# Window attention on one core: softmax over half sequences, keys without padding, rstd per sequence

## What is computed

```python
def _L1_attn_ref(x, wq, wk, wv, wo, q_norm_w, k_norm_w):
    DIM, H, KV, HD, WIN = (128, 16, 4, 64, 64)
    def rmsnorm(x, w, eps=1e-06):
        return x * jax.lax.rsqrt(jnp.mean(x * x, axis=-1, keepdims=True) + eps) * w
    q = rmsnorm((x @ wq.T).reshape(B, T, H, HD), q_norm_w)
    k = rmsnorm((x @ wk.T).reshape(B, T, KV, HD), k_norm_w)
    v = (x @ wv.T).reshape(B, T, KV, HD)
    k = jnp.repeat(k, rep, axis=2); v = jnp.repeat(v, rep, axis=2)
    scores = jnp.einsum('bqhd,bkhd->bhqk', q, k) / jnp.sqrt(jnp.float32(HD))
    mask = (i >= j) & (i - j < WIN)
    attn = jax.nn.softmax(jnp.where(mask, scores, -jnp.inf), axis=-1)
    y = jnp.einsum('bhqk,bkhd->bqhd', attn, v).reshape(B, T, H * HD)
    return y @ wo.T
```

## Time and profile before

| | |
|---|---|
| median of 3 runs | 2810.6 us (2810.01 to 2815.29) |
| the profiled execution | 2811.5 us, its span 2809.7 us |
| mean granted TensorE clock | 0.949 |
| busy over the span: PE, PEld | 2401.2 us (85%), 1568.5 us (56%) |
| busy over the span: DVE, ACT, POOL | 2138.4 (76%), 1455.2 (52%), 1191.9 us (42%) |
| the window attention layer | about 1754 to 2272 us of the span |

### The profile page before, as it was taken

One profiled execution on the slowest core, in us unless ns is written; L12 is line 12 of the kernel. 1 busy time (PEld: TensorE's weight loads), 2 busy tenths in 40 slices (PEclk: granted clock), 3 DMA queues, 4 the chain that ended last, 5 costly groups with the idle time before them and its releaser, 6 DMA issues. The chain is left out here.

```text
span 2809.7 us, 46598 instructions
## 1 busy us (share of the span) xinstructions
PE 2401.2 (85%) x14880; PEld 1568.5 (56%) x14880; DVE 2138.4 (76%) x3085; ACT 1455.2 (52%) x2617; POOL 1191.9 (42%) x864
## 2 busy tenths in 40 slices
PE   2778878778887877799779999699999989978997
PEld 0233333333333332577578888466666767767776
DVE  3899999999999999577555555588888867764555
ACT  2666666666666774466332222466666646642010
POOL 4566667666666667333300000455555533231000
PEclk9899999999999999899789999899999999988999
DMA  2000000000000000200000000000000010000000
GB/s 84 1 0 0 1 0 1 1 1 0 0 0 0 0 1 0 63 12 12 22 1 1 1 0 0 6 0 0 0 0 0 1 48 11 11 4 1 11 7 12
DMA packets 35414, 22.17 MB, mean 8 GB/s; under 512 B 22710, under 2 KB 34017, under 8 KB 34801
## 3 DMA queue, kind: packets, MB, share of 16 engines
q1 hardware_dynamic: 35312, 20.98, 2.9%
HBM read 18.87 MB, written 2.10 MB: 7 GB/s over the span
## 5 line engine op out<-in xcount | busy, mean ns | idle before, releaser
L784 POOL TENSOR_TENSOR m_hc<-m_h,m_cs 128x1024 f32<-128x1024 f32 x256 | 603.2, 2359 | 351.9 <-DVE m_h L706 344.6
L706 DVE TENSOR_TENSOR_SCAN m_h<-m_da,m_pdb 128x1024 f32<-128x1024 f32 x256 | 585.1, 2286 | 23.5 <-DVE m_pdb L661 5.0
L456 PE MATMUL m_py<-m_hc,ident 128*128 128x512 f32 x1024 | 514.6, 627 | 4.2 <-DVE m_y L670 2.1
L579 ACT ACTIVATE m_da<-m_dt,m_aneg 128x508 f32<-128x508 f32 x512 | 337.8, 709 | 47.8 <-POOL m_dt L753 46.1
L661 DVE TENSOR_TENSOR m_pdb<-m_du,m_pdb 128x1024 f32<-128x1024 f32 x256 | 314.8, 1230 | 42.7 <-POOL m_du L760 11.4
L456 PEld LDWEIGHTS m_py<-m_hc,ident 128*128 128x128 f32 x1024 | 202.2, 200 | 213.6 <-issue 174.6
L594 ACT ACTIVATE m_cs<-m_pc 128x512 f32<-128x512 f32 x256 | 150.5, 588 | 219.7 <-PE m_pc L446 219.6
L442 PE MATMUL m_pdb<-m_bcrow,m_sel 96*128 96x512 bf16 x256 | 101.8, 397 | 171.8 <-DVE m_h L706 170.8
L1391 ACT ACTIVATE c_act_of<-c_pg 128x512 f32<-128x512 f32 x144 | 86.2, 598 | 237.3 <-PE c_pg L212 237.3
L1759 POOL TENSOR_TENSOR d_pr<-d_pr,d_rden 128x512 f32<-128x512 f32 x128 | 133.3, 1041 | 177.2 <-DVE d_rden L1690 177.2
L1037 ACT ACTIVATE x_prT<-x_pt 77x512 f32<-77x512 f32 x256 | 137.8, 587 | 130.6 <-PE x_pt L939 129.5
(11 more groups left out here) (257 smaller groups left out, 5373.7 us busy)
## 6 DMA issues: line engine op xcount, KB each, us to landing
cw_gu<-in_C_gu SPq DMA_DIRECT2D x1, 2304.0 KB
x<-in_x SPq DMA_DIRECT2D x8, 256.0 KB, 4.9
fw_w<-in_F_w SPq DMA_DIRECT2D x1, 2048.0 KB
out_x<-x SPq DMA_DIRECT2D x8, 256.0 KB, 2.3
bm_mrow<-in_B_mrow SPq DMA_DIRECT2D x1, 1232.0 KB, 6.5
x_ctxT<-in_B_ctxT SPq DMA_DIRECT2D x32, 38.5 KB, 1.8
x_mask<-in_B_mrow SPq DMA_DIRECT2D x32, 38.5 KB, 2.8
x_ctxT<-in_E_ctxT SPq DMA_DIRECT2D x32, 38.5 KB, 1.8
```

Source lines behind the costliest of these rows:

```text
L456: ins = mm(py[:, c, :], S.ident[:, :], hc[n % BUF][:, place(n, c), :], start=n == 0, stop=n == NS - 1)
L579: A_(dst, src, ACT.Exp, scale=aneg[:, d, c, n:n + 1]).then_inc(s["da_ready"], 1)
L706: V.tensor_tensor_scan(h[n % BUF][:, way], da[n % BUF][:, d:d + CH * GT][:, way], pdb[:, b:b + 2, :].rearrange("p c t -> p (c t)")[:, way] ...
L784: P.tensor_tensor(hc[n % BUF][:, :, :], h[n % BUF][:, :].rearrange("p (c t) -> p c t", c=CH), bc(cs[n % BUF][:, :], 1, CH), ALU.mult).then ...
```

## The change

The layer is rewritten with halves (8 heads) in place of quads.

- **Softmax by half sequences.** Maximum, subtraction, exp, sum, reciprocal and normalization work on 128 x 1024 elements, twice per sequence. pr becomes four buffers of 1024, top, den and rden two of 8 columns.
- **Scores in row tiles.** kT is copied in one instruction without padding. ps is one tensor of two banks, both used by each half: heads in rows 0 to 63 go to bank 0, heads in rows 64 to 127 to bank 1, eight products of 64 rows and 128 columns per half, the two row halves in turn. Scores of a half wait for the subtraction of the half before it.
- **Transposes** of a half are two quads in a row through the one bank pt; the copies go to four prT buffers. Values: four products per half into one py bank, one copy to cT.
- **Order.** TensorE's slot: transposes of half u - 2, values of u - 3, then in even slots the transpose of xh; in odd slots transposes of keys and queries, output projection, input projection; scores of half u + 1 last. Keys are projected and transposed before queries.
- **rstd of the heads** in two parts (keys with the first 8 query heads: 12 columns; the other 8), each with its own sum, mean and power.
- **Layer norm.** VectorE aggregates mean and variance (32 bn_aggr, first four ahead), GpSimd takes the power of one column per sequence.
- **v** is copied by GpSimd (a product with ones), not by VectorE.

Core of the diff:

```diff
-        kT = [A.sb(f"kT{p}", [128, KVL, 2, T]) for p in range(2)]
-        ps = [A.ps(f"ps{k}", [128, QH, T]) for k in range(2)]
+        kT = [A.sb(f"kT{p}", [128, KVL, T]) for p in range(2)]
+        ps = A.ps("ps", [128, 2, QH, T])
...
+                def turn(u):
+                    pe.wait_ge(s["norm_ready"], u.k + 1)
+                    for k in range(2):
+                        if due(2 * u.k + k):
+                            pe.wait_ge(s["prT_ready"], 2 * u.k + k)
+                        for i in range(QH):
+                            ins = tr(pt[:, i, :], pr[u.p][u.h][:, QH * k + i, :], S.ident[:, :])
+                        ins.then_inc(s["pt_mm"], 1)
...
+                def scores(u):
+                    if u.h == 0:
+                        pe.wait_ge(s["kT_ready"], u.n + 1)
+                    pe.wait_ge(s["qT_ready"], u.k + 1)
+                    if due(u.k):
+                        pe.wait_ge(s["sub_ready"], u.k)
+                    for k in range(2):
+                        mm(ps[:, k, :, :], S.ident_bf[:, :], bc(outside[:, :], 1, QH), start=True, stop=False)
+                    for i in range(QH):
+                        for k in range(2):
+                            half = slice(64 * k, 64 * k + 64)
+                            ins = mm(ps[:, k, i, :], qT[u.p][half, QH * u.h + i, :],
+                                     kT[u.p][half, 2 * u.h + i // 2, :], start=False, stop=i == QH - 1)
+                    ins.then_inc(s["s_mm"], 1)
...
+                def slot(u):
+                    o, m, n = u.seq.plus(-2), u.seq.plus(1), u.seq.plus(2)
+                    if u.plus(-2).real():
+                        turn(u.plus(-2))
+                    if u.plus(-3).real():
+                        values(u.plus(-3))
+                    if u.h == 0 and n.real():
+                        turn_x(n)
+                    if u.h == 1:
+                        if m.real():
+                            turn_kq(m)
+                        if o.real():
+                            project_out(o, n)
                         if n.real():
+                            project_in(n)
+                    if u.plus(1).real():
+                        scores(u.plus(1))
```

More of the change, by code:

```diff
@@ L1471, in window_attention_layer @@
         kscale = A.sb("kscale", [128, 1])
+        one = A.sb("one", [128, 1])
+        mv = A.sb("mv", [128, NB, 2])
+        ve = A.sb("ve", [128, NB])
         xh = A.sb("xh", [128, 1, D])
@@ L1542, in slot @@
[L1542 to L1581, removed]
-                        if n.real():
[L1583 to L1589, removed]
@@ new lines, in values @@
+                def values(u):
+                    pe.wait_ge(s["prT_ready"], 2 * (u.k + 1))
+                    if u.h == 0:
+                        pe.wait_ge(s["v_ready"], u.n + 1)
+                    if due(u.k):
+                        pe.wait_ge(s["cT_ready"], u.k)
+                    for e in range(2):
+                        for k in range(2):
+                            ins = mm(py[64 * k:64 * k + 64, e, :], v[u.p][:, 2 * u.h + e, :],
+                                     prT[u.h][k][:, 2 * e:2 * e + 2, :], start=True, stop=True)
+                    ins.then_inc(s["y_mm"], 1)
@@ L1593, in _ @@
+                walk_halves(pe, slot, 3)
             @block.scalar
@@ L1596, in _, with slot @@
                 act.wait_ge(s["kscale"], 2)
-                act.wait_ge(s["kT_zero"], 2)
-                def slot(b, q):
-                    y = b if q >= 2 else b.plus(-1)
+                def slot(u):
+                    e, t, y = u.plus(-1), u.plus(-2), u.plus(-3)
+                    m, n = u.seq.plus(1), u.seq.plus(2)
+                    if e.real():
+                        act.wait_ge(s["sub_ready"], e.k + 1)
+                        buf = pr[e.p][e.h]
+                        A_(buf[:, :, :], buf[:, :, :], ACT.Exp).then_inc(s["exp_ready"], 1)
+                    if t.real():
+                        for k in range(2):
+                            act.wait_ge(s["pt_mm"], 2 * t.k + k + 1)
+                            if k == 0 and due(t.k - 1):
+                                act.wait_ge(s["y_mm"], t.k - 1)
+                            A_(prT[t.h][k][:, :, :], pt[:, :, :], ACT.Copy).then_inc(s["prT_ready"], 1)
@@ L1749, in _, with slot @@
                 P = nc.gpsimd
-                for part, cols in enumerate(LN_PARTS):
-                    S.ln_scalars(pool, s["rstd"], LN_EPS, cols, part * LN_STEPS)
-                def slot(b, q):
-                    d = b if q < 3 else b.plus(1)
+                P.memset(one[:, :], 1.0).then_inc(s["one_ready"], 1)
+                pool.wait_ge(s["one_ready"], 1)
+                def slot(u):
+                    d = u.plus(-1)
+                    m, r4 = u.seq.plus(1), u.seq.plus(4)
+                    if u.h == 0 and m.real():
+                        for k in range(2):
+                            pool.wait_ge(s["ms_ready"], 2 * m.n + k + 1)
+                            if k == 0 and due(m.n):
+                                pool.wait_ge(s["kn_ready"], m.n)
+                            if due(2 * (m.n - 1) + k + 1):
+                                pool.wait_ge(s["qn_ready"], 2 * (m.n - 1) + k + 1)
+                            P.tensor_tensor(r[:, PARTS[k]], mean_sq[:, PARTS[k]], S.minus_half[:, PARTS[k]], ALU.pow
+                                            ).then_inc(s["r_ready"], 1)
@@ L1772, in _ @@
-                walk_sequences(pool, slot, 3)
+                    if u.h == 1 and u.real():
+                        pool.wait_ge(s["v_early_ready"], u.n + 1)
+                        if due(2 * (u.n - 1)):
+                            pool.wait_ge(s["y_mm"], 2 * (u.n - 1))
+                        P.tensor_tensor(v[u.p][:, :, :], v_early[u.p][:, :, :],
+                                        one[:, :].unsqueeze(2).to_broadcast([128, KVL, HDL]), ALU.mult
+                                        ).then_inc(s["v_ready"], 1)
@@ L1775 @@
+                    if u.h == 1 and r4.real():
+                        i = bass.ds(r4.n, 1)
+                        pool.wait_ge(s["ve_ready"], 1 if isinstance(r4.n, int) and r4.n < EARLY else 2)
+                        P.tensor_tensor(S.rstd[:, i], ve[:, i], S.minus_half[:, 0:1], ALU.pow
+                                        ).then_inc(s["rstd"], 1)
+                walk_halves(pool, slot, 3)
 LO = 32
```

296 lines of the change are left out of this document (139 added, 157 removed).

## The result

The changed kernel takes **2846.5 us** (median of 4 runs, 2840.63 to 2846.84) against 2812.94 us for the kernel before in the same comparison: ratio 1.0115, 95% interval 1.0096 to 1.0133, +34 us. The forecast was 2845. The profiled execution took 2846.7 us (span 2844.9). The residual sums of VectorE, one per sequence, answer to the earlier trace rows.

The account below looks back on a forecast made before the run. A loop over TensorE, VectorE and ScalarE was to bind, 16.4 us a sequence against 14.94: periods +40.5, filling -9, start +0.6, draining +2.4, so +34 us and about 2845 us (own range 2825 to 2862; with rivals 2800 to 2869).

Parts of the forecast that it names:

- the ring: Steady loop: odd exp done 2.2 us, VectorE's subtraction 6.2, odd scores 7.8, then TensorE's odd slot 8.62; period 16.4.
- TensorE's own sum: TensorE's work per sequence in the changed window attention, copy waits included: 14.86 us.
- The second quad: Second transpose quad of a half waits for ScalarE's copy of pt: starts 1.36 us after the first, 0.93 waiting.
- The wait before the odd mask: TensorE idles 1.5 us before the mask of odd halves, until VectorE's subtraction releases it.
- The normalization: GpSimd's normalizing of 1024 elements per row: 2.08 us, or 2.36 by mamba's product of that width.
- the third path: Two powers, then the odd half's normalization on GpSimd, ending at 7.5 to 7.8 us, as TensorE turns that half at 7.8.
- 28 of them at 0.12 to 0.17: Layer start: 28 VectorE aggregations behind the first four put the first xh at about +0.6 us.
- The filling: First to fifth projection: intervals of 11.4, about 13, 14.5 and 16.4 us, 55 for 64.5, so -9 us.
- The draining: Last four sequences: slots of 16.4 and 10.9, then last turns, values and outputs 11.7; 39 us, +2.4.
- A: Rival: loop does not close, TensorE's 14.86 us sets the period; 2803 us, chance 0.13.
- B: Rival: score row tiles do not overlap, +1.7 us a period; 2890 us, chance 0.05.
- C: Rival: TensorE idle 3.5 us of a period, granted clock falls to a mean of 0.9; 2872 us, chance 0.1.

Follow-up runs that it names:

- experiment 2: Changed kernel with the values placed between the two quads of a turn in odd slots alone: 2815.5 us, ratio 1.0004, period 15.55.
- experiment 4: Changed kernel with exp, sum, reciprocal and normalization of the odd half moved ahead of the next sequence's squares: 2815.5 us, ratio 1.0009, period 15.52.
- experiment 6: Changed kernel with the odd half's softmax ahead of the squares and values between the quads in both slots: 2788.6 us, ratio 0.9914, period 14.61.
- experiment 1: Changed kernel with the values placed between the two quads of a turn in even slots alone: 2865.8 us, ratio 1.0191.
- experiment 3: Changed kernel with only the exp of the odd half moved ahead of the squares on ScalarE: 2844.2 us, ratio 1.0116, period 16.458.
- experiment 5: Changed kernel with padded keys and full 128-row products as before the change, halves and order kept: 2861.6 us, ratio 1.0177, period 17.01.
- experiment 8: Changed kernel with early odd softmax, values between quads in both slots, and VectorE's odd-half sum ahead of the residual sum: 2784.4 us, ratio 0.9904.
- experiment 7: Changed kernel with early odd softmax, values between quads in both slots, and padded keys with full products: 2832.2 us, ratio 1.0064, period 15.84.

## Why the prediction was right

**What binds**: right. The period of 16.4 us was measured as 16.44 to 16.46, on the path that was named. The points of the ring were given as 2.2, 6.2 and 7.8 us and came at 2.0 to 2.2, 6.1 and 7.8. Experiments 2, 4 and 6 shorten the ring where it was said to lie, and the period follows by what they cut. In experiment 1 the undisturbed periods stay at 16.46, though TensorE's own sum is 0.9 shorter. Experiment 3 shows that the exp alone doesn't hold the loop. Exp ended 0.2 earlier than I had, but the sum starts at 2.2 all the same, behind the second mean square.

**The terms**, each as forecast and then as measured. The second quad starts 1.36 us after the first: 1.42 and 1.35. A half's row-tiled products take 1.16: 1.10. The wait before the odd mask is 1.5: 1.22. Exp of 1024 elements takes 1.03: 1.058. The powers take 2.29 and 1.67: 2.279 and 1.636. The normalization takes 2.08 to 2.36: 1.896, below both. The two widths, 1041 ns for 512 and 1896 for 1024, leave some 0.19 us that is paid once an instruction, and 2.08 counted it twice. With that the third path was weaker than I said: the normalization of the odd half ends at 2010.36, 0.67 us before TensorE transposes it. Whether it would bind by itself was not tried apart.

**The ends of the layer** are where terms were mis-sized. "28 of them at 0.12 to 0.17": the 28 aggregations take 1.94 us, and the start gained 1.9 where I had +0.6. The row of 168 ns that I took is the length of one instruction, and such instructions overlap. The trace of before had the right row, in the layer behind this one. Here it stands, and then that of the changed kernel:

```profile
2272.89 2.02 DVE L1062 BATCH_NORM_AGGREGATE x_mv<-bn 128x2 f32<-128x6 f32 x28
```

```profile
1758.54 1.94 DVE L1666 BATCH_NORM_AGGREGATE d_mv<-bn 128x2 f32<-128x6 f32 x28
```

The filling gained 6.9, not 9: its intervals were to be 11.4, 13, 14.5 and 16.4 us and are 11.1, 12.8, 17.3 and 16.5, so the third was too low by 2.8. I did not see that the output projection now stands before the input projection in its slot, which brings the first residual sum 4.5 us closer to the fifth projection. The draining was to take 39 us and takes 41.8: the last two turns, values and output projections took 14.4 where I had 11.7. The sum of these is -8.0 against -6.0 forecast, and the layers ahead, whose text is the same, differ by +2.5. So that the total came within 2 us of the forecast is luck: errors of -2.5, +2.1, -4.5 and +2.9 us at the ends, and +2.5 ahead of the layer, nearly cancel. The +40.5 of the periods is not.

**The rivals.** A (2803) needed the odd masks not to wait; they wait 1.22 us. B (2890) needed products in single file, sixteen passes at 0.107 us or 1.71 in all; they take 1.10. The Trainium skill, TensorEngine Tiling (Array Packing), Performance Considerations, says that the evacuation of PSUM may become the limit once tiles speed TensorE up. TensorE does wait for VectorE's subtraction and ScalarE's copy after the change. But experiment 5 has the same two waits without row tiles, 0.82 and 0.69 to 0.77 us, so they come from the order and the buffers and not from the tiles, and the tiles still gain 0.55 us a period, 15 us. C (2872) is absent from this kernel, whose clock stays at 1.00 with idle pieces of 0.77, 1.22 and 0.69 us in a period. In experiment 1, with about the same sum in pieces of 2.21 and 0.69, its mechanism appeared, and gave 2865.8. I had tied it to the sum of the idle time, and these runs point to the longest piece.

## What to carry over

When engines hand one buffer round, add up the ring from hand-over to hand-over, and not the busy times. An engine that drops from full to 86% busy can be the sign of a longer period. Before shortening a step, see what ends beside it, and move all of the tied steps together; here the reorderings of experiments 6 and 8 turned a loss of 34 us into a gain of 28, with no instruction less. Splitting a wait into pieces, or filling it, can pay though the ring gets no shorter by it, where TensorE's clock hangs on the wait: here it was worth 22 us.

## What was unexpected of the hardware

- TensorE's granted clock fell in 12 of 28 periods with one unbroken wait of 2.15 to 2.21 us each (0.91 over such a period). It stayed at 1.00 in the steady periods of every other kernel here, whose waits are 1.3 us at most, and 1.45 to 1.55 in experiment 7. Between 1.55 and 2.15 no run says anything. Eight useless transposes made the kernel 22 us faster.
- A VectorE tensor_scalar of 128 x 12 took 0.74 us on average instead of 0.17 while GpSimd multiplied 128 x 1024. It is not slowed by a factor but held to the end of GpSimd's instruction: it took 0.34 us (experiment 8), 0.71 (6), 0.75 (4) and 1.00 (7), and ended each time 0.02 to 0.03 us after the normalization (in the rows of 7, at 2021.01 after 2020.98). Sums of 768 elements beside the same work kept their 0.95 us, and a tensor_scalar of 128 x 8 beside GpSimd's power kept its 0.17. The Trainium skill, GPSIMD Engine Reference, Specifications, says that GpSimd shares its SBUF interfaces with VectorE and contends with instructions of a two-port mode or with two SBUF inputs. The runs agree that some instructions are struck and others not. The one that is struck has one SBUF tensor as input, so of the two cases it can only be the first; its mode no run shows.
- 28 bn_aggr of 0.15 us each were done in 1.94 us, 0.07 apiece, as small VectorE instructions overlap when none waits for the one before. The length of one is no measure of what a row of them costs.
